# An attention stage with single-bank fills for the score maxima, two-bank exponentials and whole-tile values

## What is computed

```python
q, kv = (split(x @ Wq), split(x @ Wkv))       # (b * H, n, DH) = 128 x 1024 x 16
q = _apply_rotary(freqs, q); kv = _apply_rotary(freqs, kv)
q = q * SCALE
att = jnp.einsum('bmd,bnd->bmn', q, kv)
attn = jax.nn.softmax(att, axis=-1)
out = jnp.einsum('bij,bjd->bid', attn, kv)
x = x + (out @ Wout + bout)
```

## Time and profile before

| | |
|---|---|
| median of three runs | 2415.57 us |
| the profiled execution's own time | 2414.75 us |
| its span, first to last instruction | 2412.9 us |
| TensorE, VectorE, ScalarE, GpSimd busy | 2064.1, 1996.3, 1495.9, 669.3 us |
| mean granted TensorE clock | 0.933 of full |

### The profile page before, as it was taken

The page is one execution under the profiler, slowest core; times in us unless marked ns, Lnnn a source line. Parts: engine busy times, 40 slices in busy tenths (PEclk is TensorE's granted clock), DMA queues, the critical chain, the costliest instruction groups (busy, mean ns, idle before and its releaser), DMA issues. The chain is left out here.

```text
span 2412.9 us, 52712 instructions
## 1 busy us (share of the span) xinstructions
PE 2064.1 (86%) x16812; PEld 1057.0 (44%) x16812; DVE 1996.3 (83%) x3156; ACT 1495.9 (62%) x2850; POOL 669.3 (28%) x848
## 2 busy tenths in 40 slices
PE   6776199999999999999999999993897139999898
PEld 3343033333333333333333333331454128888798
DVE  7887299999999999999999999953676787888874
ACT  4444068888888888888888888880333013443333
POOL 7887000000000000000000000001675035566664
PEclk9999589999999999999999999996898559999999
DMA  3676512222222222222222222206673023333332
GB/s 102 221 226 198 150 28 58 56 60 60 59 59 60 60 60 60 60 60 60 60 55 56 57 55 56 60 30 136 220 249 128 0 84 68 93 83 81 85 67 29
DMA packets 128508, 207.85 MB, mean 86 GB/s; under 512 B 16935, under 2 KB 89130, under 8 KB 128426
## 3 DMA queue, kind: packets, MB, share of 16 engines
q1 hardware_dynamic: 116142, 189.84, 27.7%
q0 software_dynamic: 12288, 17.05, 4.3%
HBM read 121.06 MB, written 84.67 MB: 85 GB/s over the span
## 5 line engine op out<-in xcount | busy, mean ns | idle before, releaser
L640 DVE TENSOR_REDUCE a_mx<-a_sm 128x2 f32<-128x1024 f32 x1024 | 1235.2, 1223 | 113.2 <-PE a_sm L588 97.2
L709 ACT ACTIVATE a_prob<-a_st 128x512 f32<-128x512 f32 x2048 | 1113.4, 597 | 164.8 <-PE a_st L551 133.2
L588 PE MATMUL a_sm<-a_k,a_q 48*128 48x512 f32 x2048 | 753.7, 457 | 57.7 <-DMA a_k<-qkv_parts 50.0
L551 PE MATMUL a_st<-a_q,a_k 50*128 50x512 f32 x2048 | 755.1, 450 | 0.0
L575 PE MATMUL a_pv<-a_prob,a_v 128*32 128x256 f32 x8192 | 655.8, 392 | 22.9 <-ACT a_oraw L716 22.3
L551 PEld LDWEIGHTS a_st<-a_q,a_k 50*128 50x128 f32 x2048 | 310.4, 185 | 404.1 <-ACT a_prob L709 391.0
L575 PEld LDWEIGHTS a_pv<-a_prob,a_v 128*32 128x32 f32 x8192 | 161.8, 108 | 401.7 <-issue 192.8
L588 PEld LDWEIGHTS a_sm<-a_k,a_q 48*128 48x128 f32 x2048 | 303.6, 188 | 70.9 <-DMA a_k<-qkv_parts 50.4
L682 POOL TENSOR_TENSOR a_v<-a_v_raw,a_zero 128x256 f32<-128x256 f32 x64 | 39.8, 622 | 926.2 <-DMA a_v_raw<-values 911.7
L1705 ACT ACTIVATE e_hT<-e_ps_h,e_b1b 128x512 f32<-128x512 f32 x128 | 88.3, 690 | 274.6 <-PE e_ps_h L1739 268.7
L1739 PE MATMUL e_ps_o<-e_w_high,e_hT_high 128*128 128x256 f32 x512 | 151.6, 296 | 29.0 <-DVE e_biased L1610 29.0
(11 more groups left out here) (149 smaller groups left out, 2403.6 us busy)
## 6 DMA issues: line engine op xcount, KB each, us to landing
qkv_parts<-p_parts SPq DMA_DIRECT2D x64, 512.0 KB
a_q<-qkv_parts SPq DMA_DIRECT2D x128, 128.0 KB, 2.7
a_k<-qkv_parts SPq DMA_DIRECT2D x128, 128.0 KB, 2.9
attended<-a_oraw SPq DMA_DIRECT2D x64, 256.0 KB, 2.8
e_w<-in_fc_dram SPq DMA_DIRECT2D x16, 1024.0 KB
token_table<-f_tab SPq DMA_DIRECT2D x8, 1056.0 KB, 8.7
p_x<-in_x_dram SPq DMA_DIRECT2D x16, 512.0 KB, 8.1
values<-p_values SPq DMA_DIRECT2D x8, 1024.0 KB, 19.7
```

The lines of the kernel that those rows point to most:

```text
L551: nc.tensor.matmul(st[:, slot % RING], kb[rows, q.buf, jt * P:(jt + 1) * P], qb[rows, q.buf, ic * CHUNK:(ic + 1) * CHUNK], start=True, sto ...
L588: mm = nc.tensor.matmul(sm[:, slot, h], qb[rows, q.buf, qt * P:(qt + 1) * P], kb[rows, q.buf, kc * CHUNK:(kc + 1) * CHUNK], start=True, st ...
L640: nc.vector.tensor_reduce(mx[:, qt, kc, :], sm[:, slot], AX.X, ALU.max, negate=True).then_inc(max_done, 1)
L709: nc.scalar.activation(prob[:, jt % 2, h, ic * CHUNK:(ic + 1) * CHUNK], st[:, slot % RING], ACT.Exp, scale=DH ** -0.5).then_inc(drained, 1)
```

## The change

PSUM is divided anew: `st` is two halves of two banks, one a head, `sm` is a ring of three single banks, `pv` stays. A key tile t is now one step. It has four units, scores of head 0 with both query halves and then of head 1, and after each unit's score matmul one maxima fill of the *other* head (512 keys, one bank). A fill waits for the reduction that emptied its bank, the one three fills back (`wait_for_bank`). A reduction covers 512 elements and there are twice as many. The first score matmul of a head waits for that head's exponential of the tile before. An exponential covers 1024 columns. Then come the values of the tile before, four matmuls of 512 columns. The turned maxima take a place in the ring of `sm` at t = 5, as an ordinary matmul with `nsplit` as the weights, and that bank is free when ScalarE has copied it. GpSimd does `split` of the next pair ahead of `place`. The waits of the loads on SP count `st_filled` in place of `filled`.

```diff
-    NG = 2 * TILES
-    TURN_AT = 12
-    TURN_FILL = 2 * TURN_AT
-    FILLS = 2 * NG + 1
-    AHEAD = NG + NG // 2
+    TURN_AT = 5
     RING = 3
-    QUARTER = CHUNK // 2
+    UNITS = 2 * HALVES
+    LEAD = TILES // 2
...
-        sm = a.ps("a_sm", [P, 2, 2, CHUNK])
-        st = a.ps("a_st", [P, RING, CHUNK])
+        st = a.ps("a_st", [P, 2, N])
+        sm = a.ps("a_sm", [P, RING, CHUNK])
         pv = a.ps("a_pv", [P, CHUNK])
...
+        def ahead_of(q, t):
+
+            return (q.plus(1), t + LEAD) if t < LEAD else (q.plus(2), t - LEAD)
+
+        TURN = None
+        units_of = [(u, 1 - u // HALVES, u % HALVES) for u in range(UNITS)]
+        tile_fills = [[(qt, u) for u in range(UNITS)] for qt in range(TILES)]
+        first_fills = sum(tile_fills, []) + tile_fills[0] + [TURN] + sum(tile_fills[1:LEAD], [])
+        pair_fills = sum(tile_fills[LEAD:] + tile_fills[:TURN_AT - LEAD], []) + [TURN] + sum(
+            tile_fills[TURN_AT - LEAD:LEAD], [])
+        all_fills = first_fills + 2 * pair_fills
+
...
+            def wait_for_bank(self, eng):
+
+                if self.at < RING:
+                    return
+                before = all_fills[self.at - RING]
+                end = self.at - RING + 1
+                if before is TURN:
+                    eng.wait_ge(rows_copied, self.upto("turns", end))
+                else:
+                    eng.wait_ge(max_done, self.upto("maxima", end))
...
-            def scores(q, u):
-
-                jt, ic, h = u // 4, u // 2 % 2, u % 2
-                slot, n = fill_of(q, u)
-                if u == 0:
+            def scores(q, jt, h, ic):
+
+                if jt == 0 and h == 0 and ic == 0:
                     pe.wait_ge(m_in, (q.n + 1) * 32)
-                if not (q.first() and slot < RING):
-
-                    pe.wait_ge(drained, n - (RING - 1))
+                if ic == 0 and not (q.first() and jt == 0):
+
+                    pe.wait_ge(exp_done, (q.n * TILES + jt - 1) * 2 + h + 1)
                 rows = head_rows(h, DATA_ROWS + CUTS)
-                nc.tensor.matmul(st[:, slot % RING], kb[rows, q.buf, jt * P:(jt + 1) * P],
-                                 qb[rows, q.buf, ic * CHUNK:(ic + 1) * CHUNK],
-                                 start=True, stop=True).then_inc(filled, 1)
-
-            def turn_maxima(q, slot, n):
+                cols = slice(ic * CHUNK, (ic + 1) * CHUNK)
+                mm = nc.tensor.matmul(st[:, h, cols], kb[rows, q.buf, jt * P:(jt + 1) * P], qb[rows, q.buf, cols],
+                                      start=True, stop=True)
+                if ic == HALVES - 1:
+                    mm.then_inc(st_filled, 1)
+
+            def turn_maxima(q, fill):
                 pe.wait_ge(n2_done, q.n + 1)
-                if not q.first():
-                    pe.wait_ge(drained, n - (RING - 1))
-                nc.tensor.transpose(st[:, slot % RING, 0:P], nsplit[:].bitcast(F32), ident[:]).then_inc(filled, 1)
-
-            def values(q, jt, part):
-
-                if jt == 0 and part == 0:
+                fill.wait_for_bank(pe)
+                nc.tensor.matmul(sm[0:2 * CUTS * TILES, fill.slot, 0:P], nsplit[:].bitcast(F32), ident[:],
+                                 start=True, stop=True).then_inc(sm_filled, 1)
+
+            def maxima(q, qt, unit, fill):
+
+                _, h, kc = units_of[unit]
+                if qt == 0 and unit == 0:
+                    pe.wait_ge(qk_in[q.buf], (q.turn + 1) * 16 * QK_LOADS)
+                fill.wait_for_bank(pe)
+                rows = head_rows(h, DATA_ROWS)
+                nc.tensor.matmul(sm[:, fill.slot], qb[rows, q.buf, qt * P:(qt + 1) * P],
+                                 kb[rows, q.buf, kc * CHUNK:(kc + 1) * CHUNK], start=True, stop=True
+                                 ).then_inc(sm_filled, 1)
+
+            def values(q, jt):
...
-                if part == 0:
-                    pe.wait_ge(drained, fill_of(q, 4 * jt + 3)[1] + 1)
-                cols = slice(part * QUARTER, (part + 1) * QUARTER)
+                pe.wait_ge(exp_done, (q.n * TILES + jt + 1) * 2)
                 for h in range(2):
                     for ic in range(HALVES):
                         row = 2 * DH * (h * HALVES + ic)
-                        start = ic * CHUNK + part * QUARTER
-                        mm = nc.tensor.matmul(pv[row:row + 2 * DH, cols], vb[:, q.buf, jt, h, :],
-                                              prob[:, jt % 2, h, start:start + QUARTER],
-                                              start=(jt == 0 and part == 0), stop=(jt == TILES - 1),
-                                              skip_group_check=True)
-                if part == 1:
-                    mm.then_inc(pv_done, 1)
-
-            def maxima(q, v, slot, h):
-
-                qt, kc = v // 2, v % 2
-                if v == 0 and h == 1:
-                    pe.wait_ge(qk_in[q.buf], (q.turn + 1) * 16 * QK_LOADS)
-                rows = head_rows(h, DATA_ROWS)
-                mm = nc.tensor.matmul(sm[:, slot, h], qb[rows, q.buf, qt * P:(qt + 1) * P],
-                                      kb[rows, q.buf, kc * CHUNK:(kc + 1) * CHUNK], start=True, stop=True)
-                if h == 0:
-                    mm.then_inc(sm_done, 1)
+                        mm = nc.tensor.matmul(pv[row:row + 2 * DH, :], vb[:, q.buf, jt, h, :],
+                                              prob[:, jt % 2, h, ic * CHUNK:(ic + 1) * CHUNK],
+                                              start=(jt == 0), stop=(jt == TILES - 1))
+                mm.then_inc(pv_done, 1)
...
-                seen = q.n * NG + AHEAD
-                for g in range(NG):
-                    ahead = q.plus(1) if g < NG // 2 else q.plus(2)
-                    v = (g + NG // 2) % NG
-                    if g == TURN_AT and q.plus(1).exists():
-                        turn_maxima(q.plus(1), *turn_of(q))
-                    scores(q, 2 * g)
-                    if ahead.exists():
-
-                        pe.wait_ge(max_done, seen + g - 1)
-                        maxima(ahead, v, g % 2, 1)
-                    scores(q, 2 * g + 1)
-                    if ahead.exists():
-                        maxima(ahead, v, g % 2, 0)
-                    if g >= 2:
-                        values(q, g // 2 - 1, g % 2)
+                for t in range(TILES):
+                    ahead, qt = ahead_of(q, t)
+                    if t == TURN_AT and q.plus(1).exists():
+                        turn_maxima(q.plus(1), turn_in(q))
+                    for h in range(2):
+                        for ic in range(HALVES):
+                            unit = h * HALVES + ic
+                            scores(q, t, h, ic)
+                            if ahead.exists():
+                                maxima(ahead, qt, unit, fill_in(q, t, unit))
+                    if t > 0:
+                        values(q, t - 1)
                     elif not q.first():
-                        values(q.plus(-1), TILES - 1, g % 2)
+                        values(q.plus(-1), TILES - 1)
...
-                dve.wait_ge(sm_done, s + 1)
-                nc.vector.tensor_reduce(mx[:, qt, kc, :], sm[:, slot], AX.X, ALU.max,
+                dve.wait_ge(sm_filled, fill.done())
+                nc.vector.tensor_reduce(mx[:, qt, kc, h:h + 1], sm[:, fill.slot], AX.X, ALU.max,
                                         negate=True).then_inc(max_done, 1)
-                if v == NG - 1:
...
-                split(q)
+                if q.plus(1).exists():
+                    split(q.plus(1))
...
-            def exp(q, u):
-                jt, ic, h = u // 4, u // 2 % 2, u % 2
-                slot, n = fill_of(q, u)
-                act.wait_ge(filled, n + 1)
-                if u % 4 == 0 and not (q.first() and jt < 2):
+            def exp(q, jt, h):
+                act.wait_ge(st_filled, (q.n * TILES + jt) * 2 + h + 1)
+                if h == 0 and not (q.first() and jt < 2):
                     act.wait_ge(pv_done, q.n * TILES + (jt - 1))
-                nc.scalar.activation(prob[:, jt % 2, h, ic * CHUNK:(ic + 1) * CHUNK], st[:, slot % RING],
-                                     ACT.Exp, scale=DH ** -0.5).then_inc(drained, 1)
+                nc.scalar.activation(prob[:, jt % 2, h, :], st[:, h], ACT.Exp, scale=DH ** -0.5).then_inc(exp_done, 1)
...
-                for u in range(2 * NG):
-                    if u == 4 and not q.first():
+                for t in range(TILES):
+                    if t == 1 and not q.first():
                         evacuate(q.plus(-1))
-                    if u == TURN_FILL and q.plus(1).exists():
-                        copy_max_rows(q.plus(1), *turn_of(q))
-                    exp(q, u)
-
-            copy_max_rows(Pair(0, 0, 0), 0, 0)
+                    if t == TURN_AT and q.plus(1).exists():
+                        copy_max_rows(q.plus(1), turn_in(q))
+                    for h in range(2):
+                        exp(q, t, h)
```

(62 more changed lines are left out.)

64 lines of the change are left out of this document (27 added, 37 removed).

## The result

The changed kernel takes **2503.82 us**, the median of 4 runs (2499.17 to 2522.71), against 2415.7 for the kernel before (4 runs, 2413.13 to 2423.36). The ratio is 1.038, with a 95% interval of 1.033 to 1.043: slower by 3.8%. The profiled execution took 2499.17 us, its span is 2497.4, against 2414.75 and 2412.9 before.

The account below looks back on a forecast made before the run. TensorE was taken to pace the pairs at 1.24 us a step. To the profiled 2414.75 us came +102.5 (pairs), +1.6 (opening) and -5.5 (end), giving 2513.4; the median, 0.8 higher, made it 2514, range 2475 to 2590.

Parts of the forecast that it names:

- opening: Opening, ahead of the pairs: 48 reductions 0.60 apart for 24 that are 1.13 apart, +1.6 us.
- pairs with maxima: The 62 and a half pairs with maxima: 22.15 us each, 1.64 more than 20.51, together +102.5 us.
- the end without maxima: Last twelve tiles, with no fourth fill: 1.90 us a tile on TensorE, 23.9 with turn and ends, or -5.5 us.
- stages behind: Code after the last copy out of `pv`: no change, 0 us.
- The chain to the fourth fill: In each tile the fourth fill waits for the first one's reduction, 0.57 + 0.69 + 0.05 = 1.31 us, stalling about 0.5.
- (d): Rival in each tile: the fourth fill's wait isn't on the path, TensorE's tile is 2.14, time 2352 us; chance 0.06.
- (e): Rival for the whole kernel: about the same time as before, through parts of (d); chance 0.03.
- (b): Rival in each tile: the value block is not shorter, 1.14 us, a tile is 2.88, time near 2588; chance 0.12.
- The minimum and the turned fill: Once a pair: the minimum, about 0.4 us, hides in VectorE's slack; the turned fill takes 0.31, at most 0.5.
- (a): Rival in the pairs: VectorE becomes the bound, reductions 0.69 to 0.70 apart, time 2548 to 2573 us; chance 0.12.
- (c): Rival in the pairs: the clock falls as TensorE idles about a sixth of each tile, 2590 us and up; chance 0.05.
- The boundary's 0.4: At each pair boundary: the values' wait for the copy out of `pv`, some 0.4 us, goes.

Follow-up runs that it names:

- one: The changed kernel with each maxima reduction over the first 256 of its 512 keys: 2356.69 us, ratio 0.972 to the kernel before.
- two: The changed kernel with each maxima reduction over 128 of its 512 keys: 2304.1 us in one run.
- four: The changed kernel with the whole value block moved to mid-tile, two tiles behind, with a third `prob` buffer: 2532.86 us, ratio 1.044 to the kernel before.
- five: The changed kernel with values in two blocks of 256 columns, after units 2 and 4: 2457.17 us, ratio 1.014 to the kernel before.
- nine: The kernel before with the values of each key tile in one whole block, at every second step: 2504.77 us, ratio 1.033.
- three: The changed kernel with each ScalarE exponential over 512 of its 1024 columns: 2511.4 us in one run.
- six: As five, with the turned fill and its copy moved to the middle of tile 5: 2461.15 us, ratio 1.018 to the kernel before.
- eight: As six, with a pair's first-tile values in one block, the minimum one reduction later and `mx` in three buffers: 2410.42 us, ratio 0.995 to before.
- ten: The kernel before with only the values of each pair's first tile in one whole block: 2414.49 us, ratio 0.997.

## Why the prediction was right, point by point

The forecast was 2514 in a range of 2475 to 2590, the measurement 2504: slower, by the mechanism forecast. Against the profiled execution the sum lay 14 us high, nearly all of it in the pairs; the misses at the end (5 us too low) and behind it (6 us too high) nearly cancel, which is luck. The sum against the profiled executions, from the start of the first scores (314.10 before, 316.64 after), the last minimum (1600.55 and 1691.71) and the last copy (1629.10 and 1719.57) to the end of the span, by the rows of after and then term by term:

```profile
1691.71 0.18 DVE L689 TENSOR_TENSOR a_nm<-a_mx 128x16 f32<-128x16 f32 x1
...
1719.57 0.59 ACT L755 COPY a_oraw<-a_pv 128x512 f32<-128x512 f32 x1 [1.19 <-PE a_pv L641]
```

| term | predicted | measured |
|---|---|---|
| opening | +1.6 | +2.5 |
| pairs with maxima | +102.5 | 1375.1 - 1286.5 = +88.6 |
| the end without maxima | -5.5 | 27.86 - 28.55 = -0.7 |
| stages behind | 0 | 777.8 - 783.8 = -6.0 |
| sum | +98.6 | +84.4 |

**The chain to the fourth fill** held: reduction 0.54 after the first load (I took 0.57), 0.69 long, load 0.05 to 0.06 later, 1.29 for 1.31. Experiments one and two show it to be the cause, one for one with the reduction's length; four and five bear it out, and nine shows the same wait in the other ring. Rivals (d) and (e), in which the fourth fill's wait isn't on the path, fall with it.

**From there to the next tile** I had 0.10 + 0.33 to the values; it is 1006.49 - 1006.06 = 0.43. The value block is 0.99 (1006.49 to 1007.48), as I had it. So rival (b) falls: two blocks of 256 columns would be 1.14. The tile is 2.71 for 2.73. These 0.02 in each of 500 tiles are 10 of the 14 us by which the pairs are shorter than I had them; most of the rest is their slow start (1375.1 - 62.5 x 21.97 = 2.0, for 1286.5 - 62.5 x 20.51 = 4.6 before).

The Trainium skill, TensorEngine Tiling (Array Packing), Tiling Modes, says that a change of mode drains TensorE. My estimate from rows by that rule alone, a tile of about 2.2, isn't contradicted: with the reduction cut to 291 ns the tile falls to 2.31, below the 2.48 of two steps. So TensorE does save at least 0.17 a tile, and the ring's wait lies on top of it. How much of the saving is fewer changes of mode and how much fewer instructions, no run separates.

**The minimum and the turned fill.** I hid the minimum in VectorE's slack and took 0.31 for the turned fill. Together they are 0.30, but divided otherwise: 0.10 in the tile with the minimum, 0.20 at the turned fill. That the sum fits is chance. The rows around them in after, to be set beside the earlier trace rows:

```profile
1010.54 0.17 DVE L689 TENSOR_TENSOR a_nm<-a_mx 128x16 f32<-128x16 f32 x1
...
1009.20 1.07 PE L641 MATMUL a_pv<-a_prob,a_v 128*32 128x512 f32 x8
1012.01 1.06 PE L641 MATMUL a_pv<-a_prob,a_v 128*32 128x512 f32 x8
1012.89 0.38 PE L616 MATMUL a_sm<-a_ident,a_nsplit 128*32 128x128 f32 x2
1014.92 1.07 PE L641 MATMUL a_pv<-a_prob,a_v 128*32 128x512 f32 x8
```

**VectorE** keeps its overlap: four reductions in 2.48 are (2.48 - 0.69) / 3 = 0.60 apart, and it idles 0.22 in each tile. Rival (a) falls. In the opening 32 of them, each behind a wait, take 19.23, again 0.60 apart:

```profile
288.19 19.23 DVE L681 TENSOR_REDUCE a_mx<-a_sm 128x1 f32<-128x512 f32 x32 [48.67 <-PE a_sm L626]
```

Two small reductions for a large one cost VectorE 0.07 (0.60 twice for 1.13). In after that costs nothing, as VectorE has slack. Once the ring's wait is gone, as in experiment five, four reductions at 0.60 make 2.4 in a tile of 2.46, and then two for one does take VectorE's slack. The rule of the Trainium skill that I weighed there (VectorE: DVE Perf Modes, the TRN2 errata) is stated for operations that read SBUF, and these read PSUM, so I had stretched it; the trace agrees in that small operations pay a fixed part more often.

**ScalarE** costs nothing in the pairs: 1021 ns for 1024 columns, and a start 0.92 after the last one. Experiment three shows it. **The boundary's 0.4** goes, as I had it: its gap is 2.70.

**The clock** stayed at 1.00 from 324.8 to 1720.8, though TensorE waits in each tile. Rival (c) falls. The Trainium skill, TensorE: Matmul & The Clock Gate, "A second HAM failure mode", describes, for a bf16 kernel, a clock that swings when small gaps come from cycling through PSUM banks; this fp32 kernel waits for a PSUM bank in each of its 500 tiles, and from 324.8 on no stretch of the pairs shows such a swing.

**What failed is the term of the end.** I took 1.90 for a tile without maxima, from TensorE alone. It takes 2.33 and 2.09 in turn, 2.21 on average:

```profile
1703.17 1.97 ACT L749 ACTIVATE a_prob<-a_st 128x1024 f32<-128x1024 f32 x2
1703.53 1.06 PE L641 MATMUL a_pv<-a_prob,a_v 128*32 128x512 f32 x8
...
1705.20 0.29 PEld L608 LDWEIGHTS a_st<-a_q,a_k 50*128 50x128 f32 x2 [0.37 <-ACT a_prob L749]
1705.30 1.94 ACT L749 ACTIVATE a_prob<-a_st 128x1024 f32<-128x1024 f32 x2 [0.15 <-PE a_st L608]
1705.86 1.07 PE L641 MATMUL a_pv<-a_prob,a_v 128*32 128x512 f32 x8
```

The scores of head 1 wait for its exponential of the tile before (1703.17 + 1.97 = 1705.14, load at 1705.20), and the values lie behind them. With four banks of scores and two exponentials of 0.92 a tile, ScalarE and its waits set the pace once the maxima are gone. Experiment three shows it: with half of each exponential this stretch takes 22.3 in place of 27.9, 5.6 less. I had left that as a remark ("with ScalarE at its upper bound this gain is nearly gone"); of my gain of 5.5, 0.7 is left. The 0.31 in each of 12 tiles are 3.7 of the 4.8 us by which this term missed.

The 6 us of the stages behind are in code that the change doesn't touch. In the twelve profiled executions of this document these stages take 777.8 to 790.9, so 6 us between two of them say nothing.

Two small sums of the prediction are off and change nothing in the forecast: the pair of rival (d) is 8 x 2.39 + 0.4 = 19.5 and not 19.6, which gives some 2349 and not 2352, and half of the way from 2514 to 2444 is 2479, not 2475.

In the experiments the step that failed, in five and six, was the slack: I carried the hidden minimum over from a tile of 2.71 to one of 2.46, where VectorE needs 2.4 for its reductions alone.

## What to carry to other kernels

Count the fills of a ring between two long blocks of TensorE work. With one more than banks, each burst here waited for the whole chain of the first (0.54 + 0.69 + 0.05), though the draining engine had idle time in every tile, and merging two blocks into one doubles that count. Before removing such a wait, add up the next engine's work per tile with its rare extras (a minimum, a copy, a turned fill): they ride on slack that the wait had made. Move a rare extra to where nobody waits for what stands behind it, before making the common step faster.

## What the runs showed of the hardware

A reduction from PSUM has a length of 684 ns for 512 elements, 419 for 256 and 291 for 128; queued ones of 512 start 0.60 apart, 0.09 before the last one's end. The exponential from PSUM takes 597 ns for 512 columns and 1021 for 1024, for the second of two started 0.92 after the first.

What I had not expected is the clock in the opening of the two kernels nearest to before. Granted clock is the last column but two, in before and then in experiment eight:

```profile
325.00:340.00 15.00, 15.00 (x145) 5.54 (x141) 14.13 (x13) 12.66 (x25) 0.46 (x2) 0.98 0.06 15
...
325.00:340.00 15.00, 15.00 (x86) 5.10 (x86) 9.08 (x15) 7.40 (x8) 0.45 (x2) 0.50 0.00 1
340.00:360.00 20.00, 19.92 (x126) 6.59 (x124) 13.53 (x22) 11.26 (x13) 0.00 (x0) 0.63 0.24 60
```

TensorE was busy throughout in both, and had done maxima at half clock ahead of it in both. Yet in eight (and in ten, until 352.5) the clock stayed at its lower level until 354.6, against 325.7 in before and 324.8 in after. From the first scores (317.4) to the last minimum (1605.7) eight takes 1288.3, which is 15 more than 62.5 x 20.37; in before the same difference is 4.6. So the late clock goes with about 11 us more in this profiled execution. That the late rise belongs to the kernel isn't shown. Among the twelve runs of eight five have a mean granted clock of 0.925 to 0.928 and take 2414 to 2422, the profiled one among them, and seven have 0.931 to 0.933 and take 2404 to 2411; the kernel before, on the same chip, ranges from 0.920 to 0.932 and from 2437 to 2413 as well. So it may as well change from one execution to the next. What decides when the clock rises isn't settled by these runs.
